# Identity products in TensorE's waits, and the third layer's first slot marks ahead of its scatter, in a four-layer network

## The chip, the core and the metric

The kernel runs on one core of a Trainium2 chip. The metric is the device time of one execution in microseconds (us). Three runs of the kernel before took 798.99, 801.33 and 802.66 us; the median, 801.33 us, is what the prediction is set against. The profile comes from a further execution.

## The reference, cut to what matters

Input is x of 4 images, 16 by 16 tokens each, 192 channels: 1024 tokens. Four layers follow one another; each adds a mixer of the normalised tokens to x and then a feed-forward stage of the tokens normalised again.

```python
x = x + _L0_conv_ref(_ln_c(x), ...)   # dilated attention over 3x3 neighbours
t = t + _L0_ffn_ref(_ln_t(t), ...)    # one of 3 experts for a whole image (top 1), gelu
x = x + _L1_conv_ref(_ln_c(x), ...)   # Fourier mixer: rfft2, two complex products, irfft2
t = t + _L1_ffn_ref(_ln_t(t), ...)    # 8 experts, top 2 per token, capacity 40, relu
x = x + _L2_conv_ref(_ln_c(x), ...)   # attention, 12 heads, relative positions
t = t + _L2_ffn_ref(_ln_t(t), ...)    # 8 experts, top 2 per token, no capacity
x = x + _L3_conv_ref(_ln_c(x), ...)   # attention, low-rank added weights
t = t + _L3_ffn_ref(_ln_t(t), ...)    # one of 3 experts for a whole image
```

Nothing of the added products enters any result.

## The kernel before, in words

Each engine has a queue of its own, written by hand, and the queues meet through semaphores. A stage is one `Block`; at its end all engines meet in a barrier. The token tiles are 8 of 128 tokens; an image is two tiles.

**Norm (L303 to L415).** `Norm.vector` computes statistics and normalises a quarter of two tiles at a time on VectorE; `Norm.tensor` (L344) waits for a quarter (`normed`), turns it with four transposes (`turn`, L356) into two banks of PSUM given by `BANKS`, and ScalarE copies the banks into `x_chan` (L391). With a gate, `route` (L365) computes the router's logits of the quarter before. Norms are numbered 0 to 7, an even number ahead of a mixer, an odd one ahead of a feed-forward stage; norm 2 belongs to the Fourier mixer, which calls only its `turn`.

**Attention (L515).** TensorE projects queries, relative positions, keys and values (L563 to L594). Then for each image and each pair of heads `look` (L771) multiplies keys by queries into banks 0 and 1, VectorE takes the maximum (L893), `score` (L785) repeats the product with the maximum taken off (L791, L792), ScalarE takes the exponential, and `mix_quad` (L820) multiplies by the values (L830). `look` of a pair waits for the maximum of the pair before, because both use banks 0 and 1, and at the first pair of a piece for the piece's queries and keys from DRAM. The first image is written out; a loop runs over the other three.

**Top-1 feed-forward (L1261), layers 0 and 3.** VectorE averages the tokens of an image, TensorE multiplies by the gate (L1335), VectorE picks the expert, SyncE reads the pick and loads the expert's weights, and TensorE computes hidden products (L1351) and output products (L1363). In layer 0 it also computes small products of low-rank weights (L229, L233, L237) between the gate and the hidden products.

**Fourier mixer (L1123).** It begins with the norm's quarters and a forward transform (L1155), and ends with norm 3 and its gate.

**Routed feed-forward (L1508), layers 1 and 2.** VectorE picks two experts per token and TensorE counts the tokens before each (L1686 to L1692). In layer 1, with capacity, TensorE gathers the tokens of all experts by products with marks of slots (L1701). In layer 2 the tokens of experts 0 and 1 are gathered by products with marks (`mark_slots`, L1959, on VectorE; `pick_rows`, L1724, on TensorE, product L1729, three buffers of marks), while GpSimd scatters all tokens' rows into DRAM (L2065) for experts 2 to 7; SyncE reads them back (L1645) once all 32 scatters are in, and TensorE turns them (L1720). Then come hidden products (L1741 to L1745) and output products (L1757) of each expert; GpSimd adds results into DRAM (L2054), and SyncE reads the sum back (L1675). Behind the experts' loop TensorE runs `table_products` (L1491) for the next attention; VectorE spreads them by `table_of_heads` (L1498, rows of L1503) and only then starts the next norm's statistics, since both stand in its queue in that order.

## Time and profile before

| | |
|---|---|
| median of three runs | 801.33 us |
| the profiled execution's own time | 792.72 us |
| its span | 791.0 us |
| outside the span | 1.7 us |
| TensorE busy with matmuls | 658.9 us (83% of the span) |
| VectorE, ScalarE, GpSimd busy | 391.7, 302.9, 227.3 us |
| mean granted TensorE clock | 0.896 |

A row of a timeline is: start in us from the span's first instruction, length in us, engine, line of the kernel, operation, what it writes and reads, and how many instructions the row merges; in brackets the engine's idle time ahead of it and what ended it. A clock of 0.50 is 1.2 GHz, 1.00 is 2.4 GHz. The profile shows the first 20.25 us at 1.00 because no level is recorded there.

### The profile page before, as it was taken

The numbers are of one execution on the slowest core, as the hardware profiler recorded it, in microseconds if no ns is written. First come the engines' busy times: TensorE is split into PE (matmuls) and PEld (weight loads), VectorE is DVE, ScalarE is ACT, GpSimd is POOL, SyncE is SP. The second block draws the span as 40 slices with busy tenths as digits, with TensorE's granted clock in tenths as the row PEclk, the third lists the DMA queues.
The fourth block names the chain that finished last, engine by engine and source line by source line (L and its number), as shares of the span: only waits on it lengthen the run. The fifth ranks groups of instructions, "written<-read, shape, count | busy, mean of one in ns | idle before, by whom it ended". The sixth has DMA issues, their size and how long they took to land. (4 is left out here: it accounts for less than half of the span.)

```text
span 791.0 us, 12867 instructions
## 1 busy us (share of the span) xinstructions
PE 658.9 (83%) x4034; PEld 553.6 (70%) x4034; DVE 391.7 (50%) x986; ACT 302.9 (38%) x604; POOL 227.3 (29%) x271
## 2 busy tenths in 40 slices
PE   4888986997996999957979983899996696998397
PEld 2576763895794899953767763799995276776296
DVE  4467736015345344323768756443443476875301
ACT  3334542323312344423445551335442354555223
POOL 5177600002000044442055300734334204540000
PEclk9989986798996999985989995899998697999599
DMA  3846721536006156533688403577763369850442
GB/s 90 197 113 162 174 56 40 121 101 144 4 1 179 43 162 164 125 50 65 170 227 220 103 17 94 168 189 188 167 132 31 83 170 227 224 105 1 108 123 70
DMA packets 94005, 95.14 MB, mean 120 GB/s; under 512 B 18881, under 2 KB 80212, under 8 KB 93944
## 3 DMA queue, kind: packets, MB, share of 16 engines
q1 hardware_dynamic: 80568, 75.11, 36.3%
q0 software_dynamic: 11712, 18.18, 11.4%
q10 hardware_dynamic: 1680, 1.28, 0.6%
q8 instruction: 24, 0.39, 0.2%
q14 instruction: 21, 0.17, 0.1%
HBM read 66.92 MB, written 27.84 MB: 120 GB/s over the span
## 5 line engine op out<-in xcount | busy, mean ns | idle before, releaser
L2054 POOL DMA_INDIRECT sum_scratch<-area,f_row_index x48 | 72.4, 1509 | 172.7 <-DVE area L1999 163.0
L893 DVE TENSOR_REDUCE neg_max<-psum 128x4 f32<-128x1024 f32 x72 | 87.9, 1221 | 29.5 <-PE psum L779 28.4
L1757 PE MATMUL psum<-w,area 128*112 128x192 f32 (+1 forms) x576 | 96.2, 326 | 0.0
L1757 PEld LDWEIGHTS psum<-w,area 128*112 128x112 f32 (+1 forms) x576 | 93.5, 183 | 0.0
L966 POOL TENSOR_TENSOR shift<-ident,neg_max 128x256 fp32r<-128x256 f32 x96 | 66.5, 704 | 85.7 <-DVE neg_max L893 58.0
L791 PE MATMUL psum<-q_parts,k_parts 128*128 128x256 f32 x288 | 79.1, 305 | 0.3
L779 PE MATMUL psum<-k_parts,q_parts 128*128 128x256 f32 x288 | 55.5, 319 | 23.4 <-DMA k_parts<-k_scratch 12.7
L792 PE MATMUL psum<-shift,ones_r 128*128 128x256 f32 x288 | 74.7, 290 | 0.0
L1857 DVE TENSOR_TENSOR q_parts<-w,q_parts 128x1536 fp32r<-128x1536 f32 x16 | 28.1, 1757 | 81.4 <-ACT q_parts L1787 81.4
L779 PEld LDWEIGHTS psum<-k_parts,q_parts 128*128 128x128 f32 x288 | 42.3, 206 | 36.3 <-DVE neg_max L893 18.1
L791 PEld LDWEIGHTS psum<-q_parts,k_parts 128*128 128x128 f32 x288 | 57.4, 199 | 10.4 <-issue 8.2
L853 ACT ACTIVATE area<-psum 128x512 f32<-128x512 f32 x96 | 52.3, 595 | 28.0 <-PE psum L792 28.0
L360 PE MATMUL psum<-ident,x_norm 128*96 128x128 f32 x128 | 26.5, 353 | 42.9 <-DVE x_norm L330 42.8
L792 PEld LDWEIGHTS psum<-shift,ones_r 128*128 128x128 f32 x288 | 57.5, 200 | 0.0
L1351 PE MATMUL psum<-x_wide,w 96*128 96x256 f32 x192 | 47.6, 411 | 9.4 <-DMA b<-in_f_b_dram 8.3
L563 PE MATMUL psum<-x_wide,l_w 96*96 96x512 f32 x96 | 49.9, 682 | 4.3 <-PEq L158 3.5
L360 PEld LDWEIGHTS psum<-ident,x_norm 128*96 128x96 f32 x128 | 17.3, 159 | 50.2 <-DVE x_norm L330 49.3
L1351 PEld LDWEIGHTS psum<-x_wide,w 96*128 96x128 f32 x192 | 39.5, 208 | 16.6 <-issue 9.1
L1815 ACT ACTIVATE area<-psum,b 128x384 f32<-128x384 f32 x48 | 27.9, 582 | 49.6 <-PE psum L1745 49.1
L1432 DVE TENSOR_TENSOR mixed<-psum,b 128x384 f32<-128x384 f32 x8 | 4.5, 557 | 77.0 <-PE psum L1363 77.0
L563 PEld LDWEIGHTS psum<-x_wide,l_w 96*96 96x96 f32 x96 | 17.7, 189 | 33.7 <-issue 33.7
L830 PE MATMUL psum<-area,v_stage 128*32 128x256 f32 x384 | 39.1, 385 | 0.0
(253 smaller groups left out, 1319.3 us busy)
## 6 DMA issues: line engine op xcount, KB each, us to landing
w<-in_f_w_dram SPq DMA_DIRECT2D x32, 576.0 KB, 4.7
w<-in_f_w_dram SPq DMA_DIRECT2D x16, 384.0 KB, 5.0
w<-in_f_w_dram SPq DMA_DIRECT2D x32, 192.0 KB, 5.5
q_parts<-q_scratch SPq DMA_DIRECT2D x32, 192.0 KB, 3.4
q_scratch<-area SPq DMA_DIRECT2D x22, 192.0 KB, 2.3
k_parts<-k_scratch SPq DMA_DIRECT2D x63, 64.0 KB, 3.1
q_parts<-q_scratch SPq DMA_DIRECT2D x32, 96.0 KB, 2.8
q_parts<-q_scratch SPq DMA_DIRECT2D x40, 64.0 KB, 3.3
```

What stands on the lines that cost most here:

```text
L360: ins = pe.transpose(net.psum[0:HC, banks[half], P * k:P * (k + 1)], net.x_norm[:, 2 * q + k, HC * half:HC * (half + 1)], net.ident[:, :])
L563: ins = pe.matmul(ps[0:HC, bank, :], m.w[:, k, D * j + HC * half:D * j + HC * (half + 1)], net.x_chan[:, k, 512 * tc:512 * (tc + 1)], star ...
L779: ins = pe.matmul(ps[:, b, IMG_TOK * c:IMG_TOK * (c + 1)], query(2 * s + b, c), k_parts[:, 2 * s + b, :], start=True, stop=True)
L791: pe.matmul(out, k_parts[:, h, keys], query(h), start=True, stop=False)
L792: ins = pe.matmul(out, net.ones_r[:, :], net.shift[:, s % 2, b, :, :], start=False, stop=True)
L830: ins = pe.matmul(ps[32 * (h % 4):32 * (h % 4 + 1), 6, 0:IMG_TOK], net.v_stage[:, k, h, :], net.probs_t[h // 2 % 3][:, h % 2, k, :], start ...
L853: act.activation(net.probs_t[s % 3][:, b, :, :].rearrange("p k t -> p (k t)"), ps[:, 2 + 2 * (s % 2) + b, :], ACT.Exp).then_inc(exp_done, 1)
L893: ins = dve.tensor_reduce(most, ps[:, 0:2, :].rearrange("p b (c k) -> p (b c) k", c=2), AX_X, ALU.max, negate=True)
L966: ins = nc.gpsimd.tensor_tensor(*shift_of(n, s, b))
L1351: ins = pe.matmul(ps[:, 3 * b + fc // 2, IMG_TOK * (fc % 2):IMG_TOK * (fc % 2 + 1)], net.w1[0:HC, b, k, P * fc:P * (fc + 1)], net.x_chan[: ...
L1757: ins = pe.matmul(ps[0:R, 6 + c // 2, D * (c % 2):D * (c % 2 + 1)], x.hidden[:, fc, R * c:R * (c + 1)], net.w2[:, b, fc, :], start=(fc == ...
L2054: pool.indirect_dma_start(net.sum_dram[:, :], bass.IndirectOffsetOnAxis(ap=row_index[0:size, b, c:c + 1], axis=0), x.y[0:size, b, c, :], N ...
```

## The change

A function `keep_busy` multiplies the identity by itself into a bank of PSUM that nobody reads, so many times. Calls of it are put at fixed places of TensorE's queue. The banks of the norm's last two quarters are others than before, so that bank 3 is free, and their waits for ScalarE's copies follow. In `look` the wait for the maximum now stands ahead of the wait for the loads. In layer 2's routing VectorE makes the first three marks of expert 0 ahead of the rows' numbers, and the places of the next round are taken down at the round's end.

```diff
+def keep_busy(net, pe, products, bank=3):
+    for _ in range(products):
+        pe.matmul(net.psum[:, bank, 0:P], net.ident[:, :], net.ident[:, :], start=True, stop=True)
+
+BETWEEN_QUARTERS = 4, 6
+AFTER_NORM = 3
+BEFORE_GATE = 14
+BEFORE_COUNT = 14
+BEFORE_ROUNDS = 9
+BEFORE_MARKS = 6
+BEFORE_EXPERT = 8
+BEFORE_WEIGHTS = 14, 34
+BEHIND_OUTPUT = 7
+BEFORE_SPECTRUM = 14
+BEHIND_EXPERTS = 44, 49
+BEFORE_LOOKS = 14
+BETWEEN_LOOKS = 6

 class Norm:
-    BANKS = (0, 1), (4, 5), (3, 6), (0, 1)
+    BANKS = (0, 1), (4, 5), (6, 0), (1, 4)
+        self.warm = n > 0
     def tensor(self, pe):
         for q in range(PAIRS_OF_TILES):
+            if q > 0 and self.warm:
+                keep_busy(net, pe, BETWEEN_QUARTERS[self.which])
             pe.wait_ge(self.normed, q + 1)
-            if q == 3:
-                pe.wait_ge(self.x_chan_ready, 2)
+            if q >= 2:
+                pe.wait_ge(self.x_chan_ready, q)
             self.turn(pe, q, self.BANKS[q])
...
+        elif self.warm:
+            keep_busy(net, pe, AFTER_NORM)

             def look(i, s):
                 n = i * PAIRS + s
+                need(pe, max_ready, n)
+                if isinstance(i, int) and s == 0 and not (m.local and i == 0):
+                    keep_busy(net, pe, BEFORE_LOOKS // (1 if i == 0 else 2), 0)
+                elif isinstance(i, int) and i == 0 and 0 < s < 3:
+                    pe.wait_ge(k_sb, 4)
+                    keep_busy(net, pe, BETWEEN_LOOKS, 7)
                 for piece, (first, _) in enumerate(PIECES):
...
-                need(pe, max_ready, n)

 # fourier_mixer, TensorE, at the block's start
+            keep_busy(net, pe, BEFORE_SPECTRUM)
 # top1_feed_forward, TensorE
+            keep_busy(net, pe, BEFORE_GATE)
             pe.wait_ge(gate_ready, 1)
...
                 prep.low_rank_products(pe)
+            keep_busy(net, pe, BEFORE_WEIGHTS[0 if prep else 1])
...
             output_products(IMGS - 1, 1)
+            if prep:
+                keep_busy(net, pe, BEHIND_OUTPUT)
 # moe_feed_forward, TensorE
+            keep_busy(net, pe, BEFORE_COUNT)
             pe.wait_ge(hot_ready, 1)
...
+                keep_busy(net, pe, BEFORE_ROUNDS)
                 pe.wait_ge(counted, 1)
...
+                    keep_busy(net, pe, BEFORE_MARKS)
                     pick_rows(r, 0)
+                    keep_busy(net, pe, BEFORE_EXPERT)
...
             each_round(pe, one_round)
+            keep_busy(net, pe, BEHIND_EXPERTS[1 if capacity is None else 0])
             table_products(net, following, pe, table_ps)
 # moe_feed_forward, VectorE, without a capacity
+                step(dve.tensor_tensor(K, A, B, ALU.add))
+                step(dve.tensor_tensor(K, K, counts[0], ALU.mult))
+                mark_slots(0, 0, last=3)
                 for k, chosen in enumerate((A, B)):
...
-                step(dve.tensor_tensor(K, A, B, ALU.add))
-                step(dve.scalar_tensor_tensor(out=K, in0=counts[0], scalar=float(slots), in1=K, op0=ALU.add, op1=ALU.mult))
...
                     dve.tensor_tensor(to_row[:, :, :], row, w, ALU.add).then_inc(rows_picked, 1)
+                    mark_slots(r, 0, first=3)
+                    low_w1(r, 0, 0)
+                    low_rows(r, 0)
...
-                    dve.wait_ge(slots_marked, START + r * (PICKED_BY_PRODUCT * TILES))
-                    step(dve.tensor_scalar(K, K, float(slots), None, ALU.subtract))
...
-                    mark_slots(r, 0)
-                    low_w1(r, 0, 0)
-                    low_rows(r, 0)
...
                 results(r, E_MOE - 1, 1)
+                if capacity is None:
+                    dve.wait_ge(slots_marked, START + (r + 1) * (PICKED_BY_PRODUCT * TILES))
+                    step(dve.tensor_scalar(K, K, float(slots), None, ALU.subtract))
+                    mark_slots(r + 1, 0, last=3)
```

`self.which` is 0 for even norms and 1 for odd ones, so that BETWEEN_QUARTERS gives 4 products to norms 4 and 6 and 6 to norms 1, 3, 5 and 7.

## Rows read from the trace of the kernel before

**Rows 1.** windows at 0.50: first:last us, length, busy of each engine, clock, DMA share, GB/s
```profile
351.34:371.82 20.48, 11.15 (x24) 4.95 (x25) 6.78 (x29) 4.61 (x13) 4.79 (x3) 0.50 0.27 67
...
733.63:750.70 17.07, 5.29 (x16) 4.22 (x15) 4.63 (x19) 3.69 (x6) 0.00 (x0) 0.50 0.49 114
sum 163.86, PE 96.34 PEld 73.17 DVE 73.14 ACT 38.39 POOL 31.71; mean PE 7.41 PEld 5.63 DVE 5.63 ACT 2.95 POOL 2.44
```

**Rows 2.** timeline, TensorE's rows: transposes at 1.00 and at 0.50, products at 1.00
```profile
107.33 1.05 PE L1044 MATMUL psum<-ident,mixed 128*96 128x128 f32 x8 [2.04 <-PEq L710]
...
114.39 1.74 PE L1044 MATMUL psum<-ident,mixed 128*96 128x128 f32 x8
...
633.81 3.73 PE L578 MATMUL psum<-area 96*96 96x128 f32 x32 [0.77 <-ACT area L607]
```

**Rows 3.** timeline from layer 1's last expert to layer 2's projection
```profile
346.33 1.10 PE L1494 MATMUL psum<-rel_pick,l_rel_rows 31*96 31x256 f32 x4
...
347.46 3.42 DVE L1503 TENSOR_TENSOR area<-psum,head_mask 96x1536 f32<-96x1536 f32 x2 [0.61 <-PE psum L1494]
...
355.55 0.62 DVE L319 BATCH_NORM_STATS2 bn<-x_res 128x6 f32<-128x192 f32 x2 [4.66 <-DMA x_res<-sum_scratch]
...
358.04 1.09 PE L360 MATMUL psum<-ident,x_norm 128*96 128x128 f32 x4 [10.62 <-DVE x_norm L330]
...
365.02 10.46 PE L563 MATMUL psum<-x_wide,l_w 96*96 96x512 f32 x16 [1.68 <-PEq L158]
```

**Rows 4.** timeline from layer 2's last expert to layer 3's projection
```profile
604.25 1.10 PE L1494 MATMUL psum<-rel_pick,l_rel_rows 31*96 31x256 f32 x4
...
614.47 0.62 DVE L319 BATCH_NORM_STATS2 bn<-x_res 128x6 f32<-128x192 f32 x2 [5.67 <-DMA x_res<-sum_scratch]
...
624.13 8.05 PE L563 MATMUL psum<-x_wide,l_w 96*96 96x512 f32 x14 [1.86 <-PEq L158]
```

**Rows 5.** timeline of norm 3 and its gate
```profile
232.97 1.04 PE L360 MATMUL psum<-ident,x_norm 128*96 128x128 f32 x8
...
237.22 2.06 PE L372 MATMUL psum<-f_gate_w,x_wide 96*128 96x8 f32 x16
```

**Rows 6.** timeline of the forward transform
```profile
186.33 10.25 PE L1155 MATMUL psum<-dft_fwd,x_norm 128*96 128x288 f32 x32 [5.67 <-DVE x_norm L330]
```

**Rows 7.** timeline of layer 1's gathering
```profile
246.42 8.73 PE L1701 MATMUL psum<-area,x_norm 128*128 128x320 f32 x20 [1.36 <-DVE area L1904]
...
247.79 1.47 ACT L1787 CAST q_parts<-w 128x1536 fp32r<-128x1536 f32 x1 [6.62 <-DMA w<-in_f_w_dram]
...
256.27 3.66 PE L1701 MATMUL psum<-area,x_norm 128*128 128x320 f32 x12 [1.12 <-DVE area L1904]
```

**Rows 8.** timeline of layer 2's routing and its first experts
```profile
477.57 3.42 PE L372 MATMUL psum<-f_gate_w,x_wide 96*128 96x8 f32 x16
...
494.00 1.06 POOL L2065 DMA_INDIRECT sorted_scratch<-x_norm,f_to_row  x1 [35.82 <-DVE f_to_row L2014]
...
494.37 0.42 DVE L1965 TENSOR_SCALAR k_parts<-f_places,f_kept 128x384 fp32r<-128x384 f32 x1
...
504.35 0.44 PE L1741 MATMUL psum<-k_parts,q_parts 128*128 128x384 f32 x1 [2.17 <-DVE k_parts L1862]
...
517.68 0.92 SPq L1645 DMA_DIRECT2D area<-sorted_scratch  x2
...
527.87 0.82 PE L1720 MATMUL psum<-ident,area 128*128 128x128 f32 x6
```

**Rows 9.** timeline of layer 0's second look
```profile
40.57 1.10 PE L779 MATMUL psum<-k_parts,q_parts 128*128 128x256 f32 x4 [2.41 <-DVE neg_max L893]
```

**Rows 10.** timeline of the top-1 stages: layer 0, then layer 3 with norm 7
```profile
140.92 9.27 PE L1351 MATMUL psum<-x_wide,w 96*128 96x256 f32 x29 [0.96 <-DVE l_w L256]
...
732.37 1.44 PE L360 MATMUL psum<-ident,x_norm 128*96 128x128 f32 x8 [1.51 <-DVE x_norm L330]
...
746.63 7.64 PE L1351 MATMUL psum<-x_wide,w 96*128 96x256 f32 x25 [7.53 <-DMA b<-in_f_b_dram]
```

More of the change, by code:

```diff
@@ L1862, in low_rows, with mark_slots @@
                 dve.tensor_tensor(x_parts[D2:P, 2, :], rows_of(e, 1), x_parts[0:D2, 2, :], ALU.subtract).then_inc(low_ready, 1)
+            def mark_slots(r, e, first=0, last=TILES):
+                if first == 0:
+                    dve.wait_ge(turned, START + job(r, e))
+                for t in range(first, last):
+                    if t >= 3:
+                        dve.wait_ge(slots_used, (r * PICKED_BY_PRODUCT + e) * (TILES - 1) + (t - 2))
+                    dve.tensor_scalar(x.is_slot[t % 3], gate.places[:, 0, :], kept[:, t, e:e + 1], None,
+                                      ALU.is_equal).then_inc(slots_marked, 1)
             dve.memset(upto[:, 1, :], 1.0)
@@ L1955, in _ @@
                 step(dve.tensor_reduce(of_pick[:, :, :, :], products[:, :, :, :, :], AX_X, ALU.add))
-                step(dve.tensor_tensor(K, A, B, ALU.add))
-                step(dve.scalar_tensor_tensor(out=K, in0=counts[0], scalar=float(slots), in1=K, op0=ALU.add, op1=ALU.mult))
-            def mark_slots(r, e):
-                dve.wait_ge(turned, START + job(r, e))
-                for t in range(TILES):
-                    if t >= 3:
-                        dve.wait_ge(slots_used, (r * PICKED_BY_PRODUCT + e) * (TILES - 1) + (t - 2))
-                    dve.tensor_scalar(x.is_slot[t % 3], gate.places[:, 0, :], kept[:, t, e:e + 1], None,
-                                      ALU.is_equal).then_inc(slots_marked, 1)
             def know_rows(r, e, b):
@@ L2002, in one_round, with next_and_this @@
             def one_round(r):
+                def next_and_this(e, b):
+                    low_w1(r, e + 1, 1 - b)
+                    low_rows(r, e + 1)
+                    know_rows(r, e, b)
+                    results(r, e, b)
                 if capacity is None:
@@ L2019, in one_round @@
                     step(dve.tensor_scalar(left[:, :, :], left[:, :, :], float(slots), None, ALU.subtract))
-                    dve.wait_ge(slots_marked, START + r * (PICKED_BY_PRODUCT * TILES))
-                    step(dve.tensor_scalar(K, K, float(slots), None, ALU.subtract))
-                def next_and_this(e, b):
-                    low_w1(r, e + 1, 1 - b)
-                    low_rows(r, e + 1)
-                    know_rows(r, e, b)
-                    results(r, e, b)
-                if capacity is None:
-                    mark_slots(r, 0)
-                    low_w1(r, 0, 0)
-                    low_rows(r, 0)
                     for e in range(1, PICKED_BY_PRODUCT):
```

## The prediction

> **What bounds the kernel now.** I read the profile's page first, then the windows by stage, then the timelines of the stages that the diff touches; the chain of waits covers only the last stage and was read for that alone. The page says that TensorE is busy 83% of the span, no other engine half as much in every stage, and that its mean clock is 0.896. The windows give 13 stretches at 0.50 behind the start, 163.86 us together, in which TensorE is busy 96.34 us [rows 1]; the reader is to see in the first and the last of them that it mostly waits there. They lie where a stage begins: TensorE had little to do, the level fell, and the next dense work starts at half speed. So what the change can win is bounded by 96.34 / 2 = 48 us, and less where something else ends the wait. What it can lose is time in which TensorE multiplies identities while real work is ready, and what stands behind the trains in its queue.
>
> **The price of a product.** No row of before shows this product. Its nearest: products of 128 columns leave two records each (32 records for 16 products of L578), 3.73 us for 32, so 0.109 us a record with the last one's tail taken off; transposes of the same width take 0.109 at 1.00 and 0.213 at 0.50, from 1.05 us and 1.74 us for eight [rows 2]. So a product costs 0.22 us at 1.00 and 0.43 at 0.50; the ends are 0.11 (one record) and 0.50. Trains: 4 are 0.87 us, 6 are 1.3, 14 are 3.0, 34 are 7.4, 44 are 9.6, 49 are 10.6.
>
> **Part by part,** plus is slower, at the place where the time is on the path.
>
> *Behind the experts, layer 1.* TensorE is done at 346.33; `table_products` 1.10 us; VectorE spreads the table from 347.46 for 3.42 us, is done at 350.9, and starts the norm at 355.55, when the sum is back from DRAM [rows 3]. The 44 products stand ahead of `table_products`. So the table comes at 346.33 + 9.6 + 1.1 = 357.0, VectorE spreads it until 360.4, and only then the statistics start: 4.9 us late. The cover of 4.7 us that the table had is gone. Then TensorE has nothing from 357.0 to 360.4 + 2.5 = 362.9, so I take the clock to fall again, as it fell in the wait of 10.62 us there before. The norm's quarters come every 1.6 us; at 0.50 four transposes and 4 products take 0.85 + 1.7 = 2.6 us, so the quarters pile up until the level rises: with a rise after some 5 us (6.8 behind the start of L563 here, 3.7 in layer 3 [rows 1, 3, 4]) it is 1.5 us more. The gain: L563 starts at 365.02 and its first 8 records, until 371.82, go at 0.85 instead of 0.43: -3.4. Sum +3.0; ends -3.4 (the table turns out not to be on the path) and +8.
>
> *Behind the experts, layer 2.* The same: TensorE done at 604.25, table at 604.25 + 10.6 + 1.1 = 616.0, spread until 619.4, statistics at 619.4 instead of 614.47: +5.0; piled-up quarters +1.5; L563 was at 0.50 from 624.13 to 627.82 only: -1.9 [rows 4]. Sum +4.6; ends -1.9 and +9.
>
> *Norm 3.* All quarters but the last are ready when TensorE arrives: eight transposes run in one piece at 232.97, and TensorE is busy nearly without a gap until 237.22 + 2.06 = 239.28 [rows 5]. Three trains of 1.3 us are 3.9; about 1.0 us of gaps takes some: +2.9 (0 to +3.9). Behind them stand the gate's products, the barrier, and all of layer 1's routing.
>
> *Norms 1, 5, 7.* Quarters come every 2.15 us and 6 products fit into that, but the last quarter follows the third at once: 1.44 us for both at 732.37 [rows 10]; with a train between, TensorE and ScalarE's last copy end later, the cold rate saved against it: +0.5 (norm 1) and +0.9 (norm 7). The products after the norm run beside that copy: 0. The two waits for `x_chan` ask for copies of quarters long taken: 0, up to +0.3.
>
> *First looks.* In layer 0 the maximum is known at 40.5 and the second look starts at 40.57 [rows 9]; the train stands between the two. The clock has just fallen there (window 37 to 41), so 6 products are 2.6 us, the next 6 are 1.3, the faster work behind gives 1.7 back: +2.2, passed on by the loads that wait for scores. In layers 2 and 3 the 14 products lie inside the wait for the keys and keep the level; then 2.6 us of trains against 1.2 saved on three looks and 0.8 on a score: +0.6, and +0.4 in layer 3. Sum +3.2 (0 to +6).
>
> *Layer 0's and 3's expert.* Gate: the 14 products fit into the mean's reduction; four records at 1.00 instead of 0.50, -0.4 each. Layer 3: 34 products end just before the weights land; L1351 then starts at 1.00 where it ran at 0.50 from 746.63 to 750.70: -2.0 [rows 1, 10]. Layer 0: the 14 stand behind the low-rank products, which ran at 0.50 throughout before, so the trace doesn't show whether they hold the higher level. If they do, L1351 starts near its old 140.92 [rows 10] and runs twice as fast: -4. If not, the train takes up to 6.0 us and pushes that start back by some 3, which the faster start just repays, or not: +3. Nearer to the second, since that is the level of the rows shown: -1.0. Sum -3.8.
>
> *Fourier.* 7 products and 14 hold the level through the barrier. L1155 takes 10.25 us for 32 records of 288 columns [rows 6]; by the price of 0.109 for 128 columns they take 32 x 0.245 = 7.85 at 1.00: -2.4. The end of nothing won stands for a level that fell in spite of both trains: -2.4 to 0.
>
> *Layer 1's routing.* Six count records faster: -0.7. The gathering runs from 246.42 to 259.93 [rows 7]; at 1.00 from its start a tile is 4 x 0.27 = 1.1 us, but ScalarE's first copy waits for its cast, which ends at 249.26, and VectorE has one of 1.75 us to make. That ends it at some 256.1 by the old starts, so -3.1 beside the -0.7. The stretch behind (262.60 to 266.01) has no train ahead of it: it stays or goes, -0.7. Sum -4.5 (-6.5 to 0).
>
> *Layer 2's routing.* The first mark was at 494.37, and expert 0's hidden products started at 504.35, with a cold stretch of 3.4 us soon behind [rows 8]. The first three marks now need only the places, not the rows' numbers nor the loop: I put them at 490, the six products ahead of the gathering end at 491, and with the other five marks one behind the other the hidden products start at 499.4: -5.0, and -1.5 for the stretch. But VectorE's three marks (3 x 0.42 = 1.2) come ahead of the rows' numbers, so the 32 scatters, which started at 494.00, start no earlier: norm 5's gate gives 1.3 back, the marks take 1.2. SyncE reads at 517.68 as before, expert 0's rows, VectorE's results and expert 2's rows follow one another to some 524.5. TensorE reached the turning of expert 2's rows at 527.87 [rows 8]; it would now be there at 521.4 and waits. So -3.4 is the most; with 3 us of nothing in it I add 1.4 for a new cold stretch. Sum -2.0 (-3.4 to +2). The marks and the subtraction at the round's end write buffers that are free and stand behind the last results, before a norm that waits for DRAM: 0; two more marks' time, +1.2, if that cover were gone.
>
> **Sum.** +3.0 +4.6 +2.9 +1.4 +3.2 -3.8 -2.4 -4.5 -2.0 = +2.4 us. Against the profiled execution: 792.72 (span 791.0 and 1.7 around it) + 2.4 = 795.1. The three runs shown are slower than it, median 801.33, and nothing in the trace says why; I carry the difference over: 803.7.
>
> A rule to weigh: the Trainium skill, "TensorE: Matmul & The Clock Gate", section Terms, puts the penalty of the throttle at the throttled time times (1 - K/N). For this trace it would be 163.86 / 2 = 82 us to win, against the 48 us that busy time in those stretches allows. The trace doesn't bear it out as a price of the span, because the engine idles through 41% of them.
>
> **Rivals.**
> A, the forecast, 0.52: gains of 12.7 us and losses of 15.1; 803.7, its own range 799.5 to 808.
> B, faster, 0.23: the trains are harmless where I see them late. If spreading the table and the piled-up quarters cost nothing (-4.9 -5.0 -3.0 = -12.9), the same gains leave 790.8; if half of it holds, 797. For it: the counts of 44 and 49 fill the waits of 10.62 and 11.6 us almost to the end. Against it: VectorE's queue has the table ahead of the statistics, and its only cover is 4.7 us [rows 3]. It decides from a statistics start earlier than 2 us behind the old one.
> C, clearly slower, 0.15: trains run at 0.50. A train at half speed is twice as long, and all that fit exactly overrun: 34 in layer 3 (+7.4), 14 ahead of the looks of layers 2 and 3 (6.0 us in a wait of 3.7, +2.3 each), the quarters of norms 4 and 6 in full (+1.7 each). One or two of these give 809 to 815. It decides from a train that starts after a wait long enough for the level to fall, as in the looks of layer 0.
> D, 0.08: little moves, since the cold work saved was not on the path and losses are as small: 801.3.
> E, 0.02: all of the 48 us comes back: 753.
>
> **How the numbers follow.** Half a per cent, 4.0 us, is about what a measurement of this kernel can tell from no change. Slower than 805.3: 0.22 of A, all of C, together 0.37. Same: 0.27 of A, 0.06 of B, 0.07 of D, together 0.40. Faster than 797.3: 0.03 of A, 0.17 of B, 0.01 of D, E, together 0.23. The range of 794 to 811 leaves out about 0.18: E and the lower part of B, the upper part of C.
>
> **What would show it.** In the changed kernel's profile: records of the identity product 0.109 apart at 1.00; L1503 at some 357 and 616 of the old times and the first statistics 4 to 5 us later than the sum's landing; no gap in TensorE in norm 3 and a later end; L1155, L1351 of layer 3 and L563 at 1.00 from their first record; the mean clock up from 0.896 to over 0.95; a wait of some 3 us ahead of the first L1720. The prediction is wrong if the statistics start when the sum lands, if the scatters' read is earlier and takes the wait before L1720 away (then -3 more), or if the level falls inside the trains.

## The result, and the profile after

The changed kernel takes 812.9 us (median of 4 runs, 809.3 to 817.3) where the one before takes 800.8 on the same chip: ratio 1.017, with a 95% interval from 1.013 to 1.021. It is slower by 12 us by the medians and by 14 by the ratio. I had predicted 803.7, with a range of 794 to 811: wrong in size, and the time lies above the range.

The page of the profiled execution (809.26 us, span 807.6). The rows are the share of each engine, then TensorE's busy share and granted clock in 40 slices.

```profile
PE 728.0 (90%) x4860; PEld 632.1 (78%) x4860; DVE 393.3 (49%) x989; ACT 301.2 (37%) x604; POOL 226.2 (28%) x271
...
PE   4888989999998999987989998799999698999997
...
PEclk9999988899999999998999999799999899999999
```

The windows of the nine stretches at 0.50 behind the start (columns as in [rows 1]):

```profile
362.31:369.13 6.82, 2.90 (x14) 2.84 (x15) 6.57 (x26) 1.52 (x5) 0.00 (x0) 0.50 0.01 2
...
sum 54.58, PE 41.56 PEld 36.18 DVE 26.61 ACT 7.17 POOL 8.10; mean PE 4.62 PEld 4.02 DVE 2.96 ACT 0.80 POOL 0.90
```

The change did what it says: 54.58 us at 0.50 are left of 163.86 [rows 1], and TensorE is busy 90% of the span, not 83%. The kernel is slower all the same. TensorE's busy time in these stretches fell from 96.34 to 41.56 us, which at full speed saves 27 us at most; what the added products cost was more. The Trainium skill, "TensorE: Matmul & The Clock Gate", section Terms, puts the penalty at throttled time times (1 - K/N), which would make the change worth (163.86 - 54.58) / 2 = 55 us. Measured, it is a loss, and the fastest kernel below, with 47.8 us left at 0.50, won 20 us and not 58. So the rule fails here as a price of the time.

Where it is lost, by stages. I call a run of added products a train. Each number is the time between two instructions that all traces have. Stretches that nothing touches (most of the Fourier mixer, the experts' loops) are left out, so a column doesn't add up to the span, but the changes do add up to the difference of the profiled executions. "Before" and "after" are the means of two traces each: the first of each kernel, and those of the first and the fifth experiment.

```
stage                                    before   after   change  predicted
start to norm 1 (layer 0's looks)        121.02  123.28    +2.3     +2.2
norm 1                                     5.05    6.05    +1.0     +0.5
layer 0's gate and expert                 55.35   54.75    -0.6     -1.4
forward transform                         15.70   13.90    -1.8     -2.4
norm 3 and its gate                        7.57   10.52    +3.0     +2.9
layer 1's routing                         33.77   31.37    -2.4     -4.5
behind the experts, layer 1               25.77   29.19    +3.4     +3.0
layer 2's attention                       91.55   92.70    +1.2     +0.6
norm 5, gate, layer 2's routing           66.77   67.86    +1.1     -2.0
behind the experts, layer 2               25.98   30.14    +4.2     +4.6
layer 3's attention                       91.61   94.00    +2.4     +0.4
norm 7                                    14.06   15.03    +1.0     +0.9
layer 3's gate and expert                 51.04   50.93    -0.1     -2.4
sum                                                       +14.5     +2.4
```

**The table.** TensorE's timeline behind layer 1's experts (L295 is the product by the identity, L1530 the table, L386 norm 4, L589 the projection), and VectorE's. They answer to [rows 3].

```profile
349.35 9.99 PE L295 MATMUL psum<-ident 128*128 128x128 f32 x88
359.27 1.10 PE L1530 MATMUL psum<-rel_pick,l_rel_rows 31*96 31x256 f32 x4
366.23 1.09 PE L386 MATMUL psum<-ident,x_norm 128*96 128x128 f32 x4 [5.86 <-DVE x_norm L352]
367.11 1.91 PE L295 MATMUL psum<-ident 128*128 128x128 f32 x8
...
374.17 5.36 PE L589 MATMUL psum<-x_wide,l_w 96*96 96x512 f32 x12 [1.27 <-PEq L158]
```

```profile
360.41 3.42 DVE L1539 TENSOR_TENSOR area<-psum,head_mask 96x1536 f32<-96x1536 f32 x2 [10.44 <-PE psum L1530]
363.75 0.60 DVE L341 BATCH_NORM_STATS2 bn<-x_res 128x6 f32<-128x192 f32 x2
```

The reader is to see that the statistics (L341) have no idle time before them now: what ends last there is no longer the DMA of the sum but the spreading of the table. 88 records in 9.92 us are 0.113 a record, 0.225 us a product. From the last output product to the statistics it is 14.56 us instead of 9.48, and 15.67 instead of 10.48 in layer 2.

**The looks.** TensorE's timeline in layer 0 and in layer 3 (L810 is the look, L779 before):

```profile
40.97 2.52 PE L295 MATMUL psum<-ident 128*128 128x128 f32 x12 [2.22 <-DVE neg_max L924]
43.14 1.20 PE L810 MATMUL psum<-k_parts,q_parts 128*128 128x256 f32 x4
45.66 1.60 PE L295 MATMUL psum<-ident 128*128 128x128 f32 x12 [1.32 <-DVE neg_max L924]
47.02 0.72 PE L810 MATMUL psum<-k_parts,q_parts 128*128 128x256 f32 x4
...
670.90 0.73 PE L810 MATMUL psum<-k_parts,q_parts 128*128 128x256 f32 x4 [0.41 <-DMA k_parts<-k_scratch]
673.48 2.93 PE L295 MATMUL psum<-ident 128*128 128x128 f32 x12 [1.84 <-DVE neg_max L924]
676.05 0.85 PE L810 MATMUL psum<-k_parts,q_parts 128*128 128x256 f32 x4
```

The wait for VectorE's maximum stands ahead of the train, not behind it: in layer 3 TensorE idles 1.84 us, the level falls at 672.92 within that wait, and then six products take 2.57 us at 0.50 while the look is ready. A train behind a wait fills nothing.

**Layer 2's second gathering.** VectorE's timeline (L1912 marks a tile's slots, three buffers, so from the fourth on a mark waits for TensorE to be done with a tile):

```profile
506.88 0.78 DVE L1912 TENSOR_SCALAR shift<-f_places,f_kept 128x384 fp32r<-128x384 f32 x2
516.34 0.42 DVE L1912 TENSOR_SCALAR k_parts<-f_places,f_kept 128x384 fp32r<-128x384 f32 x1 [8.68 <-remote]
519.16 0.42 DVE L1912 TENSOR_SCALAR shift<-f_places,f_kept 128x384 fp32r<-128x384 f32 x1 [2.40 <-PE psum L1767]
521.98 0.42 DVE L1912 TENSOR_SCALAR shift<-f_places,f_kept 128x384 fp32r<-128x384 f32 x1 [2.40 <-PE psum L1767]
523.41 0.42 DVE L1912 TENSOR_SCALAR k_parts<-f_places,f_kept 128x384 fp32r<-128x384 f32 x1 [1.01 <-remote]
```

TensorE's last product of the first tile of that gathering:

```profile
511.77 0.34 PE L1767 MATMUL psum<-k_parts,tokens_low 128*64 128x384 f32 x1
```

The first tile's last product is recorded at 511.77 for 0.34 us, and the mark that waits for it starts at 516.34, 4.2 us behind its end. In the first trace of before the same two marks of the second gathering stand 0.70 apart:

```profile
512.13 0.42 DVE L1965 TENSOR_SCALAR k_parts<-f_places,f_kept 128x384 fp32r<-128x384 f32 x1 [6.78 <-PE psum L1729]
512.83 0.42 DVE L1965 TENSOR_SCALAR shift<-f_places,f_kept 128x384 fp32r<-128x384 f32 x1 [0.28 <-PE psum L1729]
```

TensorE's signals come late here, and VectorE and TensorE wait for one another; I call this the stall. No term of mine had it. The experiments below follow it. (GpSimd's scatters beside it are 16, two for each of 8 tiles. The 32 that stand in my account of the kernel and in the prediction are wrong.)

### The profile page after: what moved, and what is told of

The parts are those of the page before. It is cut to its first block and busy times, and to the rows that moved or that the text cites. A ratio compares the mean times of both kernels' runs of the same rounds, so it can differ in the third digit from the quotient of the medians.

```text
span 807.6 us, 14559 instructions
## 1 busy us (share of the span) xinstructions
PE 728.0 (90%) x4860; PEld 632.1 (78%) x4860; DVE 393.3 (49%) x989; ACT 301.2 (37%) x604; POOL 226.2 (28%) x271
## 5 line engine op out<-in xcount | busy, mean ns | idle before, releaser
L295 PE MATMUL psum<-ident 128*128 128x128 f32 x826 | 108.3, 289 | 12.5 <-DVE neg_max L924 7.4
L295 PEld LDWEIGHTS psum<-ident 128*128 128x128 f32 x826 | 103.2, 204 | 15.2 <-DVE neg_max L924 8.7
L822 PE MATMUL psum<-q_parts,k_parts 128*128 128x256 f32 x288 | 75.9, 296 | 0.4
L823 PE MATMUL psum<-shift,ones_r 128*128 128x256 f32 x288 | 71.7, 282 | 0.0
L810 PE MATMUL psum<-k_parts,q_parts 128*128 128x256 f32 x288 | 52.1, 303 | 12.9 <-DMA k_parts<-k_scratch 7.3
L822 PEld LDWEIGHTS psum<-q_parts,k_parts 128*128 128x128 f32 x288 | 54.5, 189 | 10.7 <-issue 8.2
L810 PEld LDWEIGHTS psum<-k_parts,q_parts 128*128 128x128 f32 x288 | 39.3, 192 | 24.7 <-DVE neg_max L924 9.1
L589 PE MATMUL psum<-x_wide,l_w 96*96 96x512 f32 x96 | 45.0, 626 | 3.4 <-PEq L158 2.7
L1385 PE MATMUL psum<-x_wide,w 96*128 96x256 f32 x192 | 43.0, 381 | 1.5 <-DMA b<-in_f_b_dram 1.5
L386 PE MATMUL psum<-ident,x_norm 128*96 128x128 f32 x128 | 22.5, 309 | 22.6 <-DVE x_norm L352 22.5
L1385 PEld LDWEIGHTS psum<-x_wide,w 96*128 96x128 f32 x192 | 36.0, 190 | 7.0 <-DMA b<-in_f_b_dram 2.4
```

What stands on the lines that cost most here:

```text
L295: pe.matmul(net.psum[:, bank, 0:P], net.ident[:, :], net.ident[:, :], start=True, stop=True)
L589: ins = pe.matmul(ps[0:HC, bank, :], m.w[:, k, D * j + HC * half:D * j + HC * (half + 1)], net.x_chan[:, k, 512 * tc:512 * (tc + 1)], star ...
L810: ins = pe.matmul(ps[:, b, IMG_TOK * c:IMG_TOK * (c + 1)], query(2 * s + b, c), k_parts[:, 2 * s + b, :], start=True, stop=True)
L822: pe.matmul(out, k_parts[:, h, keys], query(h), start=True, stop=False)
L823: ins = pe.matmul(out, net.ones_r[:, :], net.shift[:, s % 2, b, :, :], start=False, stop=True)
L1385: ins = pe.matmul(ps[:, 3 * b + fc // 2, IMG_TOK * (fc % 2):IMG_TOK * (fc % 2 + 1)], net.w1[0:HC, b, k, P * fc:P * (fc + 1)], net.x_chan[: ...
```

## The experiments

All ratios are to the kernel before on the same chip. My theory after the result: (1) the trains ahead of the table cost about 10 us by the late statistics; (2) the trains between the looks stand on the path; (3) TensorE's late increments in layer 2 are a matter of their own. Rivals: the new order of marks makes the stall, or the load of the array does; the trains of the table are harmless and other trains cost.

**The changed kernel again** (no edit).

> The changed kernel once more. Its first trace had a stall of some 9.6 us in layer 2's second gathering: from 509 to 522 TensorE's signals came later than its records and the granted clock allow (five products of 384 columns 1.45 and 2.1 us apart instead of 0.87, then four 2.8 us apart instead of 0.70). Theory L (a slowdown of TensorE below its granted clock that falls on some executions and some places): the stall is gone from this place or sits elsewhere, the profiled execution is at 799 to 803 us without one and 809 with one, and times of single executions spread by 8 us. Rival M (the new order of the marks makes it): the same stall at the same place, 809 again. Ratio to before 1.012 to 1.020 by both.

812.3 us, ratio 1.018 (1.014 to 1.021). The stall is at the same place: from expert 0's first hidden product to the last product of the second gathering 20.36 us, against 20.31. Theory L's form of a chance event falls, M's stands so far.

**The table first.**

```
+            table_products(net, following, pe, table_ps)
             keep_busy(net, pe, BEHIND_EXPERTS[1 if capacity is None else 0])
-            table_products(net, following, pe, table_ps)
```

> The trains behind the experts (44 and 49 products) stand behind the products of the table of heads instead of ahead of them; nothing else changes. My theory (the train delays the table, the table's spreading by VectorE holds the statistics 5.1 and 5.2 us back, measured in the first trace): both statistics start when the sum lands, the clock stays at 1.00 through norm and projection, so some 10 us less than the changed kernel (ratio to before 1.00 to 1.006). Rival (the train itself overruns the sum's landing, or the piled-up quarters are what counts): at most 3 us less.

799.3 us, ratio 1.001 (0.998 to 1.004): 13 us less than the changed kernel. TensorE's timeline and VectorE's in this kernel:

```profile
349.43 1.10 PE L1530 MATMUL psum<-rel_pick,l_rel_rows 31*96 31x256 f32 x4
350.45 10.09 PE L295 MATMUL psum<-ident 128*128 128x128 f32 x88
361.20 0.64 PE L386 MATMUL psum<-ident,x_norm 128*96 128x128 f32 x4 [0.65 <-DVE x_norm L352]
```

```profile
350.56 3.42 DVE L1539 TENSOR_TENSOR area<-psum,head_mask 96x1536 f32<-96x1536 f32 x2 [0.61 <-PE psum L1530]
358.70 0.62 DVE L341 BATCH_NORM_STATS2 bn<-x_res 128x6 f32<-128x192 f32 x2 [4.72 <-DMA x_res<-sum_scratch]
```

The statistics wait for the DMA again, and the same 44 products now reach to 0.65 us ahead of the norm's first transposes. The two stretches at 0.50 in the norms are gone. From the last output product to the ninth record of the projection it is 22.55 us, against 29.19 (after) and 25.77 (before), and 23.82 in layer 2, against 30.14 and 25.98. So the late statistics cost more than 5 us each: they also opened a new wait of 5.86 us in which the level fell. That the place of the trains made this loss is shown. The gain of 13 us is more than the 10 I had expected; 12.9 of it lie in these two stages.

**Trains only, and marks only.** The first keeps all products by the identity and has VectorE's order of before; the second empties the loop of `keep_busy`.

> The changed kernel with the marks, the places and the round's order of before: only the products by the identity, the banks and the two waits of the norm are left of the change. My theory: layer 2's routing loses its gain of 5 us ahead of expert 0 but also the later scatters, so it ends within 3 us of the changed kernel without a stall: ratio to before 1.007 to 1.015. Rival M (the new order of the marks makes the stall of 9.6 us): no stall in layer 2's second gathering in any trace, ratio to before 1.000 to 1.008.

> The changed kernel with no product by the identity at all: what is left is the new order of marks on VectorE, the banks and the two waits of the norm. My theory: the gathering starts earlier and TensorE then waits for the rows of the third expert, whose scatters come later by the marks put ahead of them (1.2 us): ratio 0.998 to 1.003. Rival M: the stall of 9.6 us is here too, ratio 1.008 to 1.015.

Trains only: 814.0 us, ratio 1.018 (1.014 to 1.023), outside what I expected of either theory. Marks only: 798.8, ratio 1.001 (0.999 to 1.003). So the whole loss is the trains'. But the traces add something on the marks. With the new order, expert 0's hidden products start 18.7 us behind the logits' maximum instead of 22.3 and 23.5, as I had predicted; and from there to the end of the second gathering it takes 20.3 us instead of 12.3 and 14.0 (in trains only, with the old order, 15.6). What the earlier marks gain, the stall takes, and nothing is left in the time.

**The kernel before again** (no edit).

> The kernel before once more, for a second trace. The first trace of before is of an execution of 792.7 us, below all 23 timed ones of the last runs (794.3 to 802.0, median 798.7); the four other traces taken so far all have a stretch in layer 2's second gathering in which TensorE works at down to a quarter of its granted speed. Theory L (the slow stretch is a state of the chip in this place, which the first trace of before happened to miss): it is in this trace too, 4 to 8 us long, and the rest agrees with the first trace within 1 us. Rival (only the changed kernels have it, and the difference of 6 us is spread over the kernel): no such stretch, layer 2's eighth tile of expert 1 ends within 1 us of its place in the first trace.

800.2 us, and its profiled execution 800.49, where the first had 792.72. VectorE's marks in the second gathering (L1965 before):

```profile
508.49 0.74 DVE L1965 TENSOR_SCALAR shift<-f_places,f_kept 128x384 fp32r<-128x384 f32 x2
514.50 0.49 DVE L1965 TENSOR_SCALAR k_parts<-f_places,f_kept 128x384 fp32r<-128x384 f32 x1 [5.27 <-PE psum L1729]
515.96 0.42 DVE L1965 TENSOR_SCALAR shift<-f_places,f_kept 128x384 fp32r<-128x384 f32 x1 [0.96 <-PE psum L1729]
517.40 0.42 DVE L1965 TENSOR_SCALAR shift<-f_places,f_kept 128x384 fp32r<-128x384 f32 x1 [1.03 <-PE psum L1729]
519.54 0.42 DVE L1965 TENSOR_SCALAR k_parts<-f_places,f_kept 128x384 fp32r<-128x384 f32 x1 [1.71 <-PE psum L1729]
```

1.45 and 2.1 us apart instead of 0.70: the kernel before has the stall too, and the trace on which I predicted had happened to miss it. From expert 0's first hidden product to the end of the second gathering it takes 14.0 us, 1.7 more than in the first trace. Of the 7.8 us between the two traces, layer 2's routing as a whole (from the logits' maximum to the first turned rows) has 3.6, layer 0 up to norm 1 has 3.0, and layer 3's start 1.1. So the rest did not agree within 1 us, as I had expected.

**The trains fitted**, with the new marks and with the old. On top of the table first:

```
-            if q > 0 and self.warm:
+            if 0 < q < 3 and self.warm and self.which_norm != 3:
...
-BEFORE_COUNT = 14
+BEFORE_COUNT = 9
...
-BEFORE_WEIGHTS = 14, 34
+BEFORE_WEIGHTS = 0, 34
...
-BETWEEN_LOOKS = 6
+BETWEEN_LOOKS = 0
```

> The trains only where the traces show them harmless: behind the table instead of ahead of it, none in norm 3 and none ahead of a last quarter, none between the looks, 9 instead of 14 ahead of the counts, none ahead of layer 0's expert. From the trace with the table first, the sites taken out cost 3.1 (norm 3), 4.4 less what norm 1 gave back (layer 0's looks), some 2 in layer 3's looks, 1 in layer 2's, 1 in norm 7 and 1 at each count. My theory: 8 us less than with the table first, ratio to before 0.988 to 0.994. Rival (the trains taken out held the clock, and stages behind them slow down again): 0.996 to 1.002.

> The same with the marks, places and order of the round as before. If the new order of marks gains what the gathering's earlier start gives (4.9 us ahead of expert 0), this is 2 to 5 us slower than with the new marks. If the gain is lost in the slow stretch and in the rows' later scatters, the two are equal within 1.5 us.

Fitted: 783.3 us, ratio 0.981 (0.978 to 0.985). With the old marks: 778.3, ratio 0.975 (0.971 to 0.979), the fastest of all, 20 us below before. Both theories missed the first number: from the table first it is 16 us, and I had expected 8 at most. What is taken out there besides the looks (norm 3, the last quarters, layer 0's expert, the counts) was tested only together. With the old marks I had expected an equal or a slower kernel; it is 5 us faster by the medians, with intervals that just touch. Of the 4.9 us between the two traces only 1.0 lies in layer 2's routing; most of the rest is in layer 0 and layer 1, where the kernels do not differ, so how much the marks are worth stays open. The sites of the fitted kernel with old marks, from its trace: last output product to the projection's ninth record 22.21 and 23.81 us (25.77 and 25.98 before); layer 1's routing 29.24 (33.77 before, but 31.88 in the fitted kernel with the new marks, whose trains there are the same); forward transform 13.90. Its page:

```profile
PE 707.2 (91%) x4652; PEld 610.4 (79%) x4652; DVE 392.5 (51%) x986; ACT 301.2 (39%) x604; POOL 227.0 (29%) x271
```

**Marks of zeros.** The comparison is with -1.0 instead of `kept[:, t, e:e + 1]`.

> The changed kernel with the marks of layer 2's first two experts all zero (the places are compared with -1), so their gathered rows and the moving operands of the gathering and of their hidden products are zeros; every instruction, wait and transfer is as in the changed kernel. Theory P (the slow stretch comes from the load of the array, which depends on data): no slow stretch, expert 1's gathering takes 5.6 us, and the kernel is 6 to 9 us faster than the changed one, ratio to before 1.005 to 1.010. Rival (contention with the scatters or a semaphore path): the slow stretch is there as before, ratio 1.015 to 1.020.

812.8 us, ratio 1.018 (1.014 to 1.021); expert 0's first hidden product to the end of the second gathering 19.84 us. The stall is there with zeros as well: theory P falls.

**One scatter.**

```
-                    for t in range(TILES):
-                        for k in range(2):
+                    for t in range(TILES - 1, TILES):
+                        for k in range(1, 2):
...
-                    sp.wait_ge(dispatched, r * (2 * TILES * DMA) + 2 * TILES * DMA)
+                    sp.wait_ge(dispatched, r * DMA + DMA)
```

> The changed kernel with 1 of the 16 scatters of layer 2's rows to DRAM (what experts 2 to 7 read there is then mostly not written; everything else stands). In the traces TensorE's increments come late from 3 to 5 us after expert 0's first hidden product until 2 us behind the last scatter, whatever the data. Theory S (the late increments need the scatters beside them): no increment later than 0.1 us in the second gathering, which takes 5.6 us, and 7 to 9 us less than the changed kernel. Rival (they come from TensorE's own dense stream, or from the weights' loads): the stretch is there as before and the time stays within 2 us of 812.

801.9 us, ratio 1.004 (1.001 to 1.006): 10 to 11 us less than the changed kernel, a little more than I had expected. VectorE's marks:

```profile
505.76 0.74 DVE L1912 TENSOR_SCALAR shift<-f_places,f_kept 128x384 fp32r<-128x384 f32 x2
511.00 0.42 DVE L1912 TENSOR_SCALAR k_parts<-f_places,f_kept 128x384 fp32r<-128x384 f32 x1 [4.49 <-PE psum L1767]
511.69 0.42 DVE L1912 TENSOR_SCALAR shift<-f_places,f_kept 128x384 fp32r<-128x384 f32 x1 [0.28 <-PE psum L1767]
512.39 0.42 DVE L1912 TENSOR_SCALAR shift<-f_places,f_kept 128x384 fp32r<-128x384 f32 x1 [0.28 <-PE psum L1767]
```

0.70 apart, and 10.71 us where the changed kernel takes 20.3. The stall needs the scatters: shown. Which part of them does it, GpSimd's work or their traffic to DRAM, is not, and SyncE's reads of the rows come earlier here too (507.22). All other 12 traces but the first of before have the stall, with 14.0 to 22.4 us in that place.

**The looks, put back and taken out.** Into the fitted kernel with old marks the 6 products ahead of the second and third look are put back; from the changed kernel they alone are taken (`BETWEEN_LOOKS = 0`).

> The fitted kernel with old marks, and only the 6 products ahead of the second and third look put back in layers 2 and 3 and the 6 between the looks of layer 0. My prediction priced these trains at +2.2 in layer 0 and at +0.6 and +0.4 in layers 2 and 3, crediting them with the faster work behind. If the credit belongs to the train ahead of the first look alone, two trains of 1.3 us cost 2.6 us each in layers 2 and 3 and over 2 in layer 0: 6 to 8 us slower than without, ratio to before 0.982 to 0.986. If the prediction's prices hold: 3 us slower, 0.977 to 0.980.

> The changed kernel without the 6 products ahead of the second and third look (layers 0, 2 and 3); all else as in the changed kernel. With them put back into the fitted kernel, the trace lost 4.4 us in layer 0, 1.6 in layer 2 and 2.4 in layer 3. If these are the trains' own price, this is 6 to 9 us faster than the changed kernel, ratio to before 1.006 to 1.010. If layer 0's part is given back by the transfers that the scores wait for, 3 to 5 us faster, 1.011 to 1.014. Rival (the prediction's price of 3.2 us for all of them, of which 2.2 in layer 0, taken back by the clock): 1 to 3 us faster.

Put back: 787.6 us, ratio 0.986 (0.982 to 0.989), so about 9 us slower than without, where the first theory said 6 to 8 and the prediction's prices 3. Taken out of the changed kernel: 801.3 us, ratio 1.005 (1.002 to 1.007), 10 us faster by the ratios and 11 to 12 by the medians, more than I had expected of any theory. TensorE's timeline in layer 3 without them:

```profile
667.79 0.74 PE L810 MATMUL psum<-k_parts,q_parts 128*128 128x256 f32 x4 [0.36 <-DMA k_parts<-k_scratch]
669.93 0.89 PE L810 MATMUL psum<-k_parts,q_parts 128*128 128x256 f32 x4 [1.40 <-DVE neg_max L924]
```

The next look stands 2.14 us behind the first; in the changed kernel these two are at 670.90 and 676.05, 5.15 us apart. From the projection's ninth record to the sixth look layer 2 takes 39.26 us (41.8 in the changed kernel, mean of two) and layer 3 38.86 (42.6): 2.5 and 3.8 us for two trains, against 2.6 for them at full speed. Up to norm 1 it is 2.9 us. These 9.2 us lie where the trains stood. Away from them this trace is 2.4 us shorter in layer 1's routing and 1.7 in layer 3's expert, and 2.1 us longer in layer 2's routing.

**No trains in the routings** (`BEFORE_COUNT`, `BEFORE_ROUNDS`, `BEFORE_MARKS`, `BEFORE_EXPERT` = 0 in the fitted kernel with old marks).

> The fitted kernel with old marks without the trains ahead of the counts of layers 1 and 2 and without the three trains of layer 2's routing. If they are worth what the traces suggest (2.2 to 2.9 us in layer 1's routing, where the stretch at 0.50 would come back, nothing in layer 2), this is 2 to 3 us slower, ratio 0.977 to 0.979. If the gain there came from the clock kept by earlier trains, it is equal.

781.0 us, ratio 0.976 (0.972 to 0.980) against 0.975 (0.971 to 0.979): 1 us slower by the ratios, less than I had expected, and the intervals overlap, so it isn't told from equal. By the traces, it takes 15.18 us instead of 12.71 from the first count to the last product of the gathering in layer 1. But the fitted kernel with new marks, which has these trains, takes 14.08, and its routing as a whole 31.88, against 31.62 without. So what the trains are worth there is not shown.

## Why the prediction was wrong

I forecast +2.4 us, and the profiled executions (means of two) moved by 14.5. Of the 12.1 us between them, 3.1 are in layer 2's routing, where the step on TensorE's arrival failed; 2.6 in the looks of layers 2 and 3, where I took off a credit that the trains between them don't earn; 2.3 in layer 3's gate and expert; 2.1 in layer 1's routing; and 2.0 spread over the small terms. The greatest costs, the trains ahead of the table, I had right.

**Right.** The price of a product (0.22; 0.225 measured). The table behind the trains: +3.0 and +4.6 predicted, +3.4 and +4.2 measured, by the mechanism named: statistics 5.1 and 5.2 us late, the level falling in the wait behind, quarters piled up. Norm 3 (+2.9; +3.0), norm 7 (+0.9; +1.0), layer 0's looks as a whole (+2.2; +2.3; this agreement is in part luck, since the two traces of before differ by 3.0 us there. Seven traces with these trains need 122.9 to 125.8 us up to norm 1, seven without them 119.0 to 122.5). L1155, L563 and layer 3's L1351 at 1.00 from their first record, and a clock above 0.95 (0.965), as the prediction said it would show.

**The looks of layers 2 and 3** (+0.6 and +0.4 predicted; +1.2 and +2.4 measured). I had the trains of 2.6 us right and took 1.2 and 0.8 off for faster looks and a faster score. That credit is had without the trains between, and so is not theirs: from the projection's ninth record to the sixth look, four kernels without them take 38.2 to 39.3 us in layer 2 (39.8 before) and 38.3 to 38.9 in layer 3 (40.2 before). What these share is the first train, the 14 products inside the wait for the keys. And in layer 3 the first train between looks ran at 0.50, 2.57 us instead of 1.3: the level fell in the wait of 1.84 us that stands ahead of it.

**Layer 1's routing** (-4.5; -2.4). I took the 14 products ahead of the counts at 3.0 us in a wait.

```profile
245.30 4.99 PE L295 MATMUL psum<-ident 128*128 128x128 f32 x28 [0.32 <-PEq L1173]
250.12 0.33 PE L1723 MATMUL psum<-f_hot,upto 128*128 128x64 f32 x2
```

They start at 245.30, the level falls at 246.25, they take 4.8 us, and the counts come 0.9 us late. The number 14 alone doesn't do that: in three other kernels with 14 products the level stays there and the counts are on time (3.10 us behind the logits' maximum, as before). With 9 they are at 3.1 to 3.2 us. The stretch behind, which I hoped to lose in part (-0.7), stayed, at 266.73. In two of those three kernels (one scatter, and no trains between looks) it is gone, and the routing takes 29.0 us, 4.8 less than before. So the step that failed is a level taken as held.

**Layer 2's routing** (-2.0; +1.1 with norm 5). Two parts of my step held: the hidden products start 4.5 us earlier behind the logits' maximum, and the scatters no earlier (0.9 us later). The step that failed is "it would now be there at 521.4 and waits": I moved TensorE's work from 504.35 to 527.87 as one piece [rows 8], at the pace of a trace that had no stall. Beside the scatters TensorE's increments come late, and what starts earlier meets more of them: from expert 0's first hidden product to the end of the second gathering it takes 20.3 us, where it took 13.2 on the mean before, so the 4.5 us are lost and 2.6 more. The gathering's end goes with the last scatter, not with its own start: in all eleven traces with late increments in the gathering it ends 4.2 to 7.4 us behind that scatter, with either order of marks. Also two parts mis-sized: norm 5 is 0.8 us longer, where I had nothing, and its gate 2.0 shorter, where I had 1.3. The wait of 3 us ahead of the first turned rows was not seen, since the gathering itself ended later.

**Layer 3's gate and expert** (-2.4; -0.1). In the first trace it is -1.4, in the second +1.2, with a stretch at 0.50 from 773 us that no train of mine explains. The 34 products are 7.7 us and end in time (L1351 starts 8.1 us behind the gate's first product, 8.6 before). Nine other traces with this train need 49.0 to 51.3 us here, against 51.0 before; my -2.4 is at the edge of them, and why they spread stays open.

**Layer 0's expert** (-1.4; -0.6) came out near the second of my two cases: its train took 5.0 us, partly at 0.50, and put the start of L1351 back by 2.1 us on the mean of the traces, and the stage behind was 2.7 us shorter. The fitted kernels without it need 52.1 and 53.6 us there, less than either: L1351 starts 4.7 us earlier than with the train, and what stands behind it is 2.8 us longer. So the train costs 1.9 us net.

**The rivals.** A's mechanism is what happened, with gains of 4.9 us instead of 12.7 and losses of 19.6 instead of 15.1. C gave the time (809 to 815) largely by luck, though part of it was there: the trains at half speed in norms 4 and 6, between the looks of layer 3, ahead of the counts and of layer 0's expert; the one that carried most of its price, layer 3's 34, was not. I had them as a case apart, with 0.15; they are a part of each term. B falls by the second experiment: the table decides, and the right place for the train was behind it.

**The median.** I carried over 8.6 us between the profiled execution and the median, since "nothing in the trace says why". That was the right size (a later median of before is 800.8), but I didn't know what it was. A second trace places 3.6 us of it in layer 2's routing, of which the stall has 1.7, and 3.0 in layer 0.

## What to carry to other kernels

A train that keeps TensorE's clock belongs behind the last instruction whose result another engine needs, and ahead of the wait, never behind it: the same 44 and 49 products cost 3.4 and 4.2 us on one side of `table_products` and won 3.2 and 2.2 on the other, and six behind a wait for VectorE cost their full length, or twice that once the level has fallen. Count what else stands in the queue, then fit the train to the wait that the trace shows, and test it site by site: of one idea, 13 us lost and 15 won (the fitted kernel, marks as in the changed one) differ only in place and number. And take two traces of the kernel before; one of 792.7 us, where the median is 800, misses what the others show.

## What the runs showed of the hardware

While GpSimd issues 16 indirect scatters (one about every 1.3 us) and TensorE multiplies without a pause beside them, TensorE's increments reach VectorE late: in the changed kernel by 4.2 us for the second gathering's first tile, and by 8.5 for its third (recorded until 513.51, its mark at 521.98). They begin to be late 2 to 7 us after expert 0's first hidden product. In all twelve traces that have the stall, the last late ones come in a burst, 0.06 to 0.07 us apart, 1.7 to 2.4 us behind the end of the last scatter, and from then on they are on time; with one scatter, and in the first trace of before, every recorded one comes within 0.02 us of its product's end. From that product to the gathering's end it is 19.8 to 22.4 us in seven traces with the new order of marks, 14.0 to 16.4 in four with the old one and 19.7 in a fifth (the looks put back, where the stall sits in expert 0's hidden products and not in the gathering), 12.3 in the first of before, and 10.7 with one scatter. VectorE's marks in the second trace of the changed kernel:

```profile
522.57 0.42 DVE L1912 TENSOR_SCALAR shift<-f_places,f_kept 128x384 fp32r<-128x384 f32 x1 [2.41 <-issue]
524.69 0.42 DVE L1912 TENSOR_SCALAR k_parts<-f_places,f_kept 128x384 fp32r<-128x384 f32 x1 [1.71 <-PE psum L1767]
525.03 0.41 DVE L1912 TENSOR_SCALAR shift<-f_places,f_kept 128x384 fp32r<-128x384 f32 x1
```

The last two need increments of two tiles, one behind the other. VectorE waits 1.71 us for the first of them and finds the second there 0.34 us later, while a tile takes TensorE at least 0.70 us. The semaphore events of this trace put three increments, of three tiles, within 0.12 us (524.67 to 524.79). So it was the signals that were late, not only the products. The Trainium skill, "TensorE: Matmul & The Clock Gate", section Seeing it yourself, warns that the clock events of a trace can be unreliable and that the gate has been seen stuck at a quarter. Marks 2.8 us apart instead of 0.70 would fit that; two within 0.34 us do not. That the stall needs the scatters is shown; by what path they hold the increments back is not, nor why the first trace of before was free of it.
